# Two-layer graph network: 34 chunks of x kept in SBUF, means folded into the centring, other gather pacing, edge rows of stage two on ACT

## What is computed

```python
h = maximum(_layernorm(x), 0)                                   # 1
# layer 0: one message per edge, summed by src
gate = silu(edge_attr @ W1.T + b1) @ W2.T + b2 + adapt_logit(type[src], type[dst])
msg  = gate * h[dst] * (cw(dist) * node_vec[dst])[:, None]
agg  = segment_sum(msg, src) / clip(segment_sum(node_vec[dst], src), 1e-8)[:, None]
y    = h + agg
x    = x + layernorm(y) * gamma + beta                          # 2
h    = maximum(_layernorm(x), 0)
# layer 1: relational, summed by dst
h1   = relu(einsum(h, weight1[rel]) + bias1);  h2 = einsum(h1, weight2[rel])
agg1 = segment_sum(h2[src] * norm, dst)
out  = x + relu(agg1 + bias2)
```

## Time and profile before

| | us |
|---|---|
| median of 3 runs | 1632.94 |
| lowest and highest of them | 1632.65, 1640.82 |
| the profiled execution, its own time | 1638.52 |
| its span in the profile | 1636.4 |

### The profile page before, as it was taken

How to read it: one execution, slowest core, us unless ns; L and a number is a source line. 1 busy time by engine, 2 the same in 40 slices (tenths; PEclk the granted TensorE clock), 3 DMA queues, 4 the chain that set the end, 5 groups by cost and what they waited for, 6 DMA issues and landing times.

```text
span 1636.4 us, 20388 instructions
## 1 busy us (share of the span) xinstructions
PE 1094.1 (67%) x5054; PEld 796.5 (49%) x5054; DVE 1357.8 (83%) x4378; ACT 608.8 (37%) x1423; POOL 1066.2 (65%) x808
## 2 busy tenths in 40 slices
PE   4888888898898898700067777777777777780000
PEld 2666666666676667500045555555555555550000
DVE  6989999999999999600599999999999999973666
ACT  2545455444444444300144444444444444440000
POOL 6656578787766555666458888888888888862000
PEclk8656666666666666555566666666666666675555
DMA  7999976666666666322556666666666666636999
GB/s 237 318 313 315 320 200 156 149 149 148 158 140 147 142 142 152 61 10 10 165 162 160 156 159 161 156 161 164 155 164 159 160 162 157 159 52 212 414 414 378
DMA packets 165337, 298.63 MB, mean 182 GB/s; under 512 B 75034, under 2 KB 91627, under 8 KB 164324
## 3 DMA queue, kind: packets, MB, share of 16 engines
q1 hardware_dynamic: 89172, 253.42, 45.8%
q0 software_dynamic: 68992, 24.64, 17.5%
q10 hardware_dynamic: 7056, 19.27, 2.9%
HBM read 209.28 MB, written 127.50 MB: 206 GB/s over the span
## 4 chain that ended last, share of the span: by engine, by line
POOL 22%; DVE 20%; DMA 18%; issue 15%; PE 9%; ACT 1%; SPq 0%; POOLq 0%; ACTq 0%; DVEq 0%
POOL agg L454 14%; DMA kept_out<-x_mid 7%; PE ps_s L549 4%; POOL agg L497 3%; POOL nodes L413 3%; DVE same L824 3%; DMA agg<-y,once 2%; DMA agg<-ysq,once 2%; DVE ynrm L1037 2%; DVE x L1042 2%; PE ps_k L623 2%; POOL t L487 2%; DMA agg<-u,once 2%; DMA agg<-ynrm,once 2%; DVE ygam L1039 2%
## 5 line engine op out<-in xcount | busy, mean ns | idle before, releaser
L497 POOL DMA_INDIRECT agg<-sums,once x196 | 336.4, 1716 | 76.9 <-issue 57.7
L549 PEld LDWEIGHTS ps_s<-msg,same 128*128 128x128 f32 x1816 | 357.1, 302 | 33.5 <-issue 31.2
L549 PE MATMUL ps_s<-msg,same 128*128 128x48 f32 (+1 forms) x1816 | 361.9, 381 | 3.2 <-DVE msg L932 2.2
L413 POOL DMA_INDIRECT nodes<-in_table,dst_all x196 | 200.3, 1022 | 105.4 <-issue 52.5
L487 POOL DMA_INDIRECT t<-agg,src_all x196 | 211.1, 1077 | 84.3 <-issue 55.8
L623 PE MATMUL ps_k<-h_t,rw_sb 56*128 56x256 f32 x588 | 116.2, 508 | 152.9 <-issue 93.6
L623 PEld LDWEIGHTS ps_k<-h_t,rw_sb 56*128 56x128 f32 x588 | 59.1, 229 | 187.1 <-issue 108.2
L535 PE MATMUL ps_k<-types_lo,low_hot 128*128 128x392 bf16 x196 | 94.9, 484 | 66.6 <-DVE low_hot L798 46.3
L636 PE MATMUL ps_m<-hid,rw_sb 128*64 128x256 f32 x588 | 135.3, 630 | 0.0
L804 DVE SCALAR_TENSOR_TENSOR t<-iota_hi,hi_all,ps_k 128x392 f32<-128x392 f32 x196 | 113.8, 617 | 1.9 <-PE ps_k L536 1.5
L604 PE MATMUL ps_t<-ident,h 128*128 128x128 f32 x98 | 26.3, 359 | 129.7 <-DVE h L1031 124.3
(11 more groups left out here) (155 smaller groups left out, 2684.7 us busy)
## 6 DMA issues: line engine op xcount, KB each, us to landing
agg<-in_both SPq DMA_DIRECT2D x14, 2758.0 KB
t<-agg SPq DMA_DIRECT2D x49, 784.0 KB
kept<-kept_out SPq DMA_DIRECT2D x49, 404.0 KB
kept_in<-kept SPq DMA_DIRECT2D x49, 404.0 KB
agg<-bias_rows SPq DMA_DIRECT2D x49, 384.0 KB
x_mid<-x SPq DMA_DIRECT2D x49, 384.0 KB
rows<-in_src_rows SPq DMA_DIRECT2D x49, 256.0 KB
rows<-in_dst_rows SPq DMA_DIRECT2D x49, 256.0 KB
```

The source lines that it names most:

```text
L413: pool.indirect_dma_start(nodes[s][:, t, :], None, table, bass.IndirectOffsetOnAxis(ap=dst_all[:, c:c + 1], axis=0)).then_inc(nodes_in[b % ...
L497: pool.indirect_dma_start(agg1, bass.IndirectOffsetOnAxis(ap=once1[b % LAG1][:, t:t + 1], axis=0), sums1[b % LAG1][:, t, :], None, compute ...
L549: last = mm(ps_s[:, t * width:(t + 1) * width], kept_same[:, at:at + P], m[:, v, :], start=(v == t), stop=(v == a + w - 1))
```

## The change

1. *x in SBUF.* Tensors that only stage one uses are allocated in a scope of their own (`stage_one`), and `x_res` is laid over them: the last 34 chunks of x (RES) are written there by DVE, in place of `x2` and the store to `x_mid`; the last stage reads them from there. SP loads the first four `x_mid` chunks before it waits for the last adds. The slots of the last stage lie in other buffers than before.
2. *Means folded.* The multiplication by -1/48 goes into a scalar_tensor_tensor with the addition, at `kept_out`, `dc`, `ec`, `msg` and stage two's centred `kept_in`. L888 goes: the sums of squares are kept as they are, and the scaling moves to the use.
3. *POOL's order in stage one.* The ring `nodes` has 34 blocks, PRERUN is 4 + 28 = 32. The window is 4 tiles in all blocks; four adds go out, then two gathers (BEHIND), so that the remaining 68 gathers are spread over 34 blocks.
4. *Edge rows of stage two on ACT.* `asq` and `arl` are four activations of 128x48 each, with the mean as bias and the sum over the row as second output; so is `sq`. `ac`, `cen`, `avar`, `arsum`'s reduction, `evar`, `armean` and L1004 are gone from DVE. `h2` is made by ACT, four rows, with `erstd` as scale and `nshift = nmean * erstd` as bias.

The core of the diff:

```diff
-AHEAD = 24
+AHEAD = 34
-FIRST = 3
+FIRST = 4
+BEHIND = 2
+RES = 34
...
+        x_res = sb("x_res", [P, RES * NR + TILES, H])
+
+        def x_rows(b):
+            if b < NBLOCK - RES:
+                return x2[b % 2][:, :, :]
+            at = (NBLOCK - 1 - b) * NR
+            return x_res[:, at:at + G, :]
...
                 sp.wait_ge(S["x2_done"], b + 1)
-                sp.dma_start(x_mid[b], x2[b % 2][:, TILES:G, :].rearrange("p r w -> p (r w)")).then_inc(x_stored[b % 2], 16)
+                if b < NBLOCK - RES:
+                    sp.dma_start(x_mid[b], x2[b % 2][:, TILES:G, :].rearrange("p r w -> p (r w)")).then_inc(x_stored[b % 2], 16)
...
+            for b in range(SLOTS):
+                load_mid(b)
             sp.wait_ge(S["added1"], 16 * COLS)
             for b in range(NBLOCK):
                 s = b % SLOTS
                 need(sp, S["out_done"], b - SLOTS + 1)
                 sp.dma_start(agg_last[s][:, :], agg1_chunks[b]).then_inc(last_in[s], 16)
-                sp.dma_start(x_last[s][:, :], x_mid[b]).then_inc(last_in[s], 16)
+                if b >= SLOTS:
+                    load_mid(b)
...
-                more = b + PRERUN
-                add0(b, 0)
-                add0(b, 1)
-                if more < NBLOCK:
-                    need(pool, S["hdst_done"], more - AHEAD + 1)
-                    need(pool, S["weight_done"], more - AHEAD + 1)
-                    gather_tile(more, 0)
-                    gather_tile(more, 1)
-                add0(b, 2)
-                add0(b, 3)
-                if more < NBLOCK:
-                    gather_tile(more, 2)
-                    gather_tile(more, 3)
+                for t in range(TILES):
+                    add0(b, t)
+                for c in range(PRERUN * TILES + BEHIND * b, PRERUN * TILES + BEHIND * (b + 1)):
+                    if c < COLS:
+                        if c % TILES == 0:
+                            room(c // TILES)
+                        gather_tile(c // TILES, c % TILES)
...
-                    act.wait_ge(S["ac_done"], a + 1)
-                    need(act, S["avar_done"], a)
-                    A(asq[:, :, :], ac[:, :, :], ACT.Square).then_inc(S["asq_done"], 1)
+                    act.wait_ge(S["amean_done"], a + 1)
+                    act.wait_ge(kept_got[a % T2S], 16 * uses(a, T2S))
+                    var_at = TILES * H + PC + G
+                    for t in range(TILES):
+                        last = A(asq[:, t, :], t2[a % T2S][:, t, 0:H], ACT.Square, bias=amean[:, t:t + 1], scale=1.0,
+                                 accum_out=kept_in[a % T2S][:, var_at + t:var_at + t + 1])
+                    last.then_inc(S["asq_done"], 1)
                     need(act, S["apc_done"], a)
-                    A(arl[:, :, :], ac[:, :, :], ACT.Relu).then_inc(S["arl_done"], 1)
+                    for t in range(TILES):
+                        last = A(arl[:, t, :], t2[a % T2S][:, t, 0:H], ACT.Relu, bias=amean[:, t:t + 1], scale=1.0,
+                                 accum_out=arsum[:, t:t + 1])
+                    last.then_inc(S["arl_done"], 1)
...
+                if 0 <= e < NBLOCK:
+                    act.wait_ge(S["nshift_done"], e + 1)
+                    need(act, S["h2t_done"], e)
+                    for t in range(TILES):
+                        last = A(h2[:, t, 0:H], x2b[e % 2][:, t, :], ACT.Relu, bias=nshift[:, t:t + 1], scale=erstd[:, t:t + 1])
+                    last.then_inc(S["h2_done"], 1)
...
-                V.tensor_scalar(rmean[:, :], rsum[:, :], -1.0 / H, None, ALU.mult).then_inc(S["rmean_done"], 1)
...
-                V.tensor_tensor(kept_out[s][:, 0:PC].rearrange("p (r f) -> p r f", r=NR), rl[s][:, :, :], cols(rmean[:, :], H),
-                                ALU.add).then_inc(S["pc_done"], 1)
+                dve.wait_ge(S["rsum_done"], b + 1)
+                V.scalar_tensor_tensor(out=kept_out[s][:, 0:PC].rearrange("p (r f) -> p r f", r=NR), in0=cols(rsum[:, :], H),
+                                       scalar=-1.0 / H, in1=rl[s][:, :, :], op0=ALU.mult, op1=ALU.add).then_inc(S["pc_done"], 1)
```

More of the change, by code:

```diff
@@ L210, in build @@
         ygam = sb("ygam", [P, G, H])
-        sums = [v[:, :, :].rearrange("p r h -> p (r h)")[:, k * TILES * AW:(k + 1) * TILES * AW].rearrange("p (t w) -> p t w", w=AW)
-                for v in (u, y, ysq, ynrm, ygam) for k in range(4)][0:LAG]
         x2 = pair_of(sb, "x2", [P, G, H])
-        x2b = sb("x2b", [P, TILES, H])
+        x2b = pair_of(sb, "x2b", [P, TILES, H])
         stat = sb("stat", [P, TILES])
-        nmean = sb("nmean", [P, TILES])
-        cen = sb("cen", [P, TILES, H])
         sq = sb("sq", [P, TILES, H])
@@ L230, in build @@
         sums1 = ring_of(sb, LAG1, "sums1", [P, TILES, H])
+        junk_l = t2[0][:, :, :].rearrange("p r w -> p (r w)")
+        junk_q = t2[1][:, :, :].rearrange("p r w -> p (r w)")
+        sums = [v[:, :, :].rearrange("p r h -> p (r h)")[:, k * TILES * AW:(k + 1) * TILES * AW].rearrange("p (t w) -> p t w", w=AW)
+                for v in (u, y, ysq, ynrm, ygam) for k in range(4)][0:LAG]
+        words = t2[2][:, :, :].rearrange("p r w -> p (r w)").bitcast(I32)
+        types_in = words[:, 0:2 * NHI]
@@ L685, in _ @@
                 need(act, kept_stored[b % 2], 16 * (b // 2))
-                A(kept_out[b % 2][:, PC:PC + G], var[:, :], ACT.Sqrt, bias=eps[:, :], scale=1.0 / H).then_inc(S["std_done"], 1)
+                A(kept_out[b % 2][:, PC:PC + G], kept_out[b % 2][:, PC + G:KEPT], ACT.Sqrt, bias=eps[:, :], scale=1.0 / H).then_inc(S["std_done"], 1)
                 if b + 1 < NBLOCK:
@@ L1030, in _ @@
                     dve.wait_ge(S["erstd_done"], e + 1)
-                    V.scalar_tensor_tensor(out=h2[:, :, 0:H], in0=cen[:, :, :], scalar=0.0, in1=cols(erstd[:, :], H), op0=ALU.max,
-                                           op1=ALU.mult).then_inc(S["h2_done"], 1)
+                    dve.wait_ge(S["nmean_done"], e + 1)
+                    V.tensor_tensor(nshift[:, :], nmean[:, :], erstd[:, :], ALU.mult).then_inc(S["nshift_done"], 1)
                 if yes:
```

310 lines of the change are left out of this document (138 added, 172 removed).

## The result

| | before | changed |
|---|---|---|
| median, us | 1631.68 | 1639.16 |
| lowest and highest, us | 1627.67, 1640.82 | 1637.03, 1646.88 |
| runs | 20 | 20 |
| the profiled execution, its own time | 1638.52 | 1638.20 |
| its span | 1636.4 | 1636.5 |

The ratio is 1.0051, with a 95% interval of 1.0038 to 1.0064: slower by 7.5 us, just at what can be told from no change. The forecast was 1618 us and faster. Nothing small happened, though: three large differences cancel. The profile of the changed kernel by stretch answers to the earlier trace rows; columns as there (busy us of PE, PE's weight loads, DVE, ACT, POOL, then PE clock, DMA share, GB/s).

What follows compares the result with a forecast made beforehand. It took POOL to bound stage one, a loop through DVE, ACT and PE stage two, and DMA the last stage. Terms: -32 + 47 - 33 = -18 us on 1638.5, less 2.5: 1618 us, range 1583 to 1672.

Steps and rivals of the forecast that it cites:

- Stage one, POOL: POOL's adds and gathers in stage one: 34 blocks at 11.15 us, adds ending at 750 us, minus 32 us.
- Stage one, DVE: DVE's end of stage one: five small multiplications fewer, ending at 678 us, hidden behind POOL.
- waits for PE may eat that: Stage one, DVE: waits for PE may eat the gain of 0.5 us at most in blocks after the first 18.
- rival (e): Folded scalar_tensor_tensor form on DVE runs at half rate: stage one gains nothing, 1650 us; chance 0.01.
- Stage two: Loop through DVE, ACT and PE grows 1.14 us a block: plus 47 us, from plus 18 to plus 92.
- (2): ACT part of stage two's loop: eight rows at p = 0.27 us from row to row, plus 1.64 us a block.
- rival (a): ACT's rows are dear, p from 0.32 up, eating both gains; at 0.39 about 1663 us; chance 0.26.
- Step (1): DVE part of stage two's loop: nshift replaces h2 and amean releases ACT earlier, minus 0.50 us a block.
- Step (3): Rest of stage two's loop, through PE to the next erstd: stays the same.
- microsecond in hand: POOL in stage two: a block without stretched instructions takes 12.5 us against the loop's 13.64.
- over 15.3: Sign of being wrong: time between two erstd in stage two under 14 or over 15.3 us.
- Last stage: Fewer x_mid chunks read: 38 chunks at DVE's 1.99 us in place of 2.89, minus 33 us.

Runs made afterwards that it cites:

- e3: The kernel before with only POOL's order of stage one changed (four adds, then two gathers, 32 blocks gathered ahead): 1610.38 us, ratio 0.981.
- e1: The changed kernel with the edge rows of stage two back on DVE: 1576.39 us, ratio 0.961.
- e8: The changed kernel with the rows on ACT, but asq, arl and sq summed by three DVE reductions: 1604.86 us, ratio 0.984.
- e6: The kernel before with ACT's first hid moved ahead of asq: 1595.92 us, ratio 0.979.
- e5: The changed kernel with ACT's first hid moved ahead of the asq and arl rows: 1560.81 us, ratio 0.956.
- e9: The changed kernel with ACT's copy of the sums moved behind ystd, the first hid still behind the rows: 1579.90 us, ratio 0.967.
- e10: e7 with only sq and h2 as rows on ACT: 1580.97 us, ratio 0.966.
- e7: The changed kernel with the edge rows back on DVE and the first hid moved ahead of asq: 1529.56 us, ratio 0.938.

## Why the prediction was wrong

**Stage one, POOL (predicted minus 32 us): right in kind, a little too cautious.** Blocks with gathers 11.03 us against 11.15; the last 15 took 9.98 in the mean with the last landing in it, 149.7 us in all where the mixture of 11.01 and 9.65 and 1.9 for the landing made 157.1. Minus 44.6 in the profiled pair. By e3 the order alone is worth 38, from first add to wide gather. The medians, with plus 78.5 and minus 33.8 for the other stages, leave minus 37.

**Stage one, DVE (predicted to end at 678): wrong, and harmless.** It ends at 690.2, 6 us later than before, not 6 earlier, although five instructions a block are gone. The lag arises in the first 18 blocks, those with the wider windows: at DVE's `msg` of block 12 the changed kernel is 1.1 us ahead, at that of block 17 3.6 us behind. I had called these blocks even. Behind them the folding should have gained up to 0.5 us a block and gained nothing: the 31 blocks after block 17 take 421.0 us before, 423.3 changed and 422.1 in e3, which has the order without the folding. From 458 to 656 us DVE is busy 184 us where it was 190, but PE 185 us where it was 178, with no more matmuls (841 and 850) and at a granted clock of 0.60 in place of 0.64. e3 has 177.8 us at 0.64, e1, with the folding, 185.5 at 0.60. The prediction's "waits for PE may eat that" fits this; why the clock is lower in the kernels with the folding is not shown. The rule of the Trainium skill that I had as rival (e), "Vector Engine (DVE) Microarchitecture Reference", section "Points that are easy to get wrong", is again not borne out: `msg` as scalar_tensor_tensor takes 0.36 us, as it did as tensor_tensor.

**Stage two (predicted plus 47 us, came plus 79): the step that failed is (2), the price p of a row.** I took p = 0.27; it is 0.32. That was the threshold that I had set for rival (a), "from 0.32 up", and this rival is what happened. Two errors lie in it, and the larger is the base. Its 0.19 came from `msg`, whose rows have a scale per partition and no bias; `asq` and `arl` have a bias per partition, and without their sums they cost 0.227 (e8). The two also differ in source (`msg` reads PSUM) and in function, so which of these makes the 0.04 is not shown. The Trainium skill, "ScalarE: Activation LUTs", section "What ACT_TABLE_LOAD costs", has the figures from which 0.227 follows as an estimate for a bias by pointer, and the trace agrees (0.91 us for four rows). I had set that figure beside the sum and trusted the row. The sum beside the output I priced from DVE's record of 82 ns; ACT's record is 187 ns long, but it pushes the next row by only 0.09, so this part was 0.01 off. Eight rows: 0.40 us a turn more than forecast, and 18 us in the stage.

Step (1) failed by less: DVE's part shrank by 0.31 us in place of 0.50, mostly because `amean` took 0.45 us and not 0.15 (below). Step (3), the rest of the turn, held at 7.05 us exactly. Together 0.59 us a turn more, over 46 turns 27 us. The microsecond in hand that the prediction gave POOL was counted with undisturbed issues; in the kernel before POOL issued almost without a pause at 13.6 us a turn (lines at e6). It did no harm here. The minus 5 for the first three blocks did not come either: the first turn grew from 12.77 to 13.31 us. With a turn of 15.38 us the prediction's own sign of being wrong ("over 15.3") was met, and DVE's idle time ahead of `erstd` was 1.69 us, not over 2.

**Last stage (predicted minus 33 us): right.** Minus 33.8. A resident chunk took 1.92 us in the mean and not 1.99, and among these chunks DVE waited for agg1 once, 0.87 us at 1592.0.

**The sum.** The chances had 0.52 on faster because p between 0.23 and 0.31 was the likeliest. 0.05 us in p took the whole gain: with p = 0.32 my own sum has plus 66 for stage two and plus 1 in all. That the measured terms cancel so nearly is chance, not something that the forecast saw. The range was said to leave out rival (e), but its 1650 lies inside. The starting point mattered too: the profiled execution of before lay 6.8 us above the median of the 20 runs, that of the changed kernel 1.0 below its own, so a pair of profiles that reads 0 stands for plus 7.5. What the prediction had right, and what e5, e6, e8 and e9 show, is the loop itself: each 0.1 us in it is worth 5 us, and work beside it (DVE's 1.6 us less, e8's 0.8 us more) is worth nothing. What it had not looked for is how cheaply the loop could be cut.

## What to carry to other kernels

Before moving work to an idle engine, ask what stands behind it in that engine's queue and who waits for that. Here ACT was idle for 37% of stage two in the end, but the rows were put just ahead of the one instruction that PE waited for; moving that instruction ahead of them (four lines) is worth 78 us, and shows that the loop, not the load, was the bound. Price a small instruction by a row with the same operands (bias or scale per partition, source, sum output), not only the same shape: at 48 columns `msg`'s rows took 0.19 us and those of `asq` 0.32.

And when a loop is cut, look for the next engine first: with the loop gone, DVE waits for POOL's gathers in e5, e9 and e10, and taking more from DVE (e10) lost some 50 us against e7.
